# Products that nobody reads in TensorE's waits, and the late queries projected ahead of the first scores

## The chip, the cores and the metric

The kernel runs on one core of a Trainium2 chip. The metric is device microseconds per execution. Before the change three runs took 763.17, 768.37 and 766.54 us, a median of 766.54.

## The reference, cut to what matters

Four batches of 256 tokens of width 256 pass two layers. Each layer is a cross-attention and a routed feed-forward block, all added to the residual `x`:

```
x = x + L0_xattn(layernorm(x), ctx, pos)   # 32 heads of 8, rotary angles on q and k
x = x + L0_ffn(layernorm(x))               # 16 experts of 128, top 2 of 2 groups, plus a shared expert of 512
x = x + L1_xattn(layernorm(x), ctx)        # 16 heads of 16, per-head layernorm of q and k, two softmaxes added
x = x + L1_ffn(layernorm(x))               # 60 experts of 176, top 4, plus a gated shared expert of 704
```

The result is the final `x`, in float32. Nothing of the computation changes.

## The kernel before, in words

Tokens are eight tiles of 128 (`NT`), and each stage is one block in which the five engines run their own programs and meet on semaphores; a stage starts when all engines have ended the one before. `ps` is the accumulator memory of eight banks, named by number.

**Preparation and first attention** share a block. `prep_l0` (L237) multiplies the context by the key and value weights (L302: two float32 products per tile, 16 in all), turns the key by its angles on VectorE and GpSimd (L362, L368, L411), then transposes (L177) and projects (L197) the eight normed tiles for the queries, and turns those in the same way. Before the third key tile TensorE waits until the first has been turned; before the third query tile (`t == 2`) it waits for the first turned query. Keys and queries are split into three bf16 parts per value (`split_tensor` L223, then ScalarE, VectorE, GpSimd), the parts are written to memory and read back as stacks, first by SyncE and the last two splits by ScalarE's queue.

`attention` (L492) serves both layers. Its first loop on TensorE computes the first eight pairs of score products (`scores`, L629), runs at most three pairs ahead of VectorE's maxima (L769), and behind the fourth pair transposes the negated maxima of the first unit (`transposed_maxima`, L642), which SyncE then puts behind the queries (L555). A product with a zero row (L733) clears bank 6. The main loop, one step per pair of heads, issues scores eight pairs ahead, the shifted scores (L659), whose exponentials ScalarE takes (L857), the values (L674) and the turned sums (`token_sums`, L687). In the last steps the normalised rows are transposed and projected (`transposed`, `projected`, through L177 and L197), and VectorE adds them to `x` with statistics (L801, L803).

**Routing and experts of the first layer** (`route_and_experts_l0`, L916): VectorE norms, TensorE transposes eight tiles (L177, two banks in turn with ScalarE's copies L190), multiplies by the router's 16 columns (L197), then runs the shared expert (L1001, L1011) and 32 units of routed experts (L1041, L1052). GpSimd squares the hidden values (L1131, L1141); ahead of its first square it waits for small loads and copies masks (L1118).

**The second attention** begins with what the first could not do earlier: the queries of the last four tiles (`LateQueries`, L1515). VectorE norms them, TensorE turns two tiles (L1538) and projects them (L197), and VectorE adds the bias and centres (L1601), sums squares (L1607), spreads and scales (L1613 to L1621); TensorE transposes the result (L1554), and VectorE takes the rest (L1467). TensorE's list interleaves this with pairs 1 and 2 of the scores; VectorE's list interleaves it with the maxima. In TensorE's program before:

```
for n in range(AHEAD * UP):
    ...
    if late is not None and 1 <= n <= 2:
        late.tensor_turned(pe, n - 1)
    scores(n, 0)
    scores(n, 1)
    if late is not None and 1 <= n <= 2:
        late.tensor_projected(pe, n - 1)
```

**Routing and experts of the second layer** (`route_shared_l1`, `routed_l1`): eight transposes of pairs (L177), the gate product of 61 columns (L197), three units of the shared expert's first product (L1874, four products of 512 columns each), one of its second (L1889, L1890), and then the ranks (L1898), which need VectorE's mask of the chosen experts (L2036). The routed experts, their loads and the final sum follow from there.

The order on every engine is written out by hand. SyncE issues almost all loads. No planner is involved.

Of the kernel before, what the change touches and what calls it, by code (L numbers as in the profile page):

```python
# [18 lines left out]
P = 128  # L19
# [22 lines left out]
def bcast(ap, axis, n):  # L42

    a = ap.unsqueeze(axis)
    shape = list(a.shape)
    shape[axis] = n
    return a.broadcast_to(shape)
# [143 lines left out]
                          m.ps[:, bank, 0:D].rearrange("p (c t) -> p c t", c=KD))  # L191


def matmul_tile(nc, out, xT, i, w, bias=None, ones=None):

    for c in range(KD):
        ins = nc.tensor.matmul(out, xT[:, c, i * P:(i + 1) * P], w[:, c, :], start=(c == 0),  # L197
                               stop=(c == KD - 1 and bias is None))
    if bias is not None:
        ins = nc.tensor.matmul(out, ones, bias, start=False, stop=True)  # L200
    return ins
# [35 lines left out]
def prep_l0(nc, m, io, block, ctx):  # L237

    lay = L0
# [53 lines left out]
    @block.tensor  # L293
    def _(pe):
        pe.wait_ge(ld_ctx, 16)
        pe.wait_ge(ld_wkv, 16)
        for i in range(NT):
            if i >= 2:
                pe.wait_ge(v_copied, i - 1)
                pe.wait_ge(rot_ready, i - 1)  # L300
            for side in range(2):
                ins = nc.tensor.matmul(ps[:, 2 * side + i % 2, 0:D], m.ctxT[:, i * P:(i + 1) * P],  # L302
                                       wkv[:, side * D:(side + 1) * D], start=True, stop=True)
            ins.then_inc(kv_ps, 1)
        pe.wait_ge(v_copied, NT)
        pe.wait_ge(ld_const, 32)
        pe.wait_ge(ld_wq, 16)
        for i in range(NT + 1):
            if i == 3:
                for s in K_SPLITS:  # L310
                    split_tensor(nc, pe, m, s, rot_done, rest_ready).then_inc(split_ps, 1)
            if i == 6:
                for s in Q_SPLITS[0:2]:
                    split_tensor(nc, pe, m, s, rot_done, rest_ready).then_inc(split_ps, 1)
            if i < NT:
                pe.wait_ge(xn_ready, i + 1)
                if i >= 2:
                    pe.wait_ge(xt_ready, i - 1)
                transpose_tile(nc, m, 2 + i % 2, m.xn[:, i, :]).then_inc(xt_ps, 1)
            if i >= 1:  # L320
                t = i - 1
                pe.wait_ge(xt_ready, t + 1)
                if t >= 2:
                    pe.wait_ge(rot_ready, NT + t - 1)
                matmul_tile(nc, ps[:, 4 + t % 2, 0:D], m.xT, t, wq).then_inc(q_ps, 1)
        for s in Q_SPLITS[2:4]:
            split_tensor(nc, pe, m, s, rot_done, rest_ready).then_inc(split_ps, 1)

# [163 lines left out]
def attention(nc, m, lay, io, block, w_dram, b_dram, v_bias=None, late=None):  # L492
# [12 lines left out]
    UP = G // 2  # L505
# [5 lines left out]
    with ExitStack() as ctx:  # L511
# [100 lines left out]
        def _(pe):  # L612
# [92 lines left out]
            def projected(i):  # L705
# [4 lines left out]
                    pe.wait_ge(out_used, i)  # L710
                matmul_tile(nc, ps[:, out_bank(i) + 1, 0:D], m.xT, i, ow).then_inc(out_ps, 1)

            for n in range(AHEAD * UP):
                if lay is L0 and n == 2:
                    pe.wait_ge(m.rest_ready, len(SPLITS))
                if late is not None and 1 <= n <= 2:
                    late.tensor_turned(pe, n - 1)
                scores(n, 0)
                scores(n, 1)
                if late is not None and 1 <= n <= 2:  # L720
                    late.tensor_projected(pe, n - 1)
                if n == UP:
                    if late is not None:
                        pe.wait_ge(late.cent, 2)
                    transposed_maxima(0)
                if late is not None and n == UP:
                    pe.wait_ge(negT_ready, 1)
                    for k in range(2):
                        late.tensor_split(pe, k)
            if late is not None:  # L730
                pe.wait_ge(late.rest_ready, 2)
            pe.wait_ge(zero_row_set, 1)
            nc.tensor.matmul(ps[:, 6, :], m.ones_row[:], zero_row, start=True, stop=True)  # L733
            pe.wait_ge(ones_ld, 16 * RT * NBUF)
            for n in range(PAIRS + TURN_LAG + 1):
                if n + AHEAD * UP < PAIRS:
                    scores(n + AHEAD * UP, 0)
                if n < PAIRS:
                    shifted_scores(n)
                if n + AHEAD * UP < PAIRS:  # L740
                    scores(n + AHEAD * UP, 1)
                if n < PAIRS:
                    if n % UP == 0 and n // UP + 1 < U:
                        transposed_maxima(n // UP + 1)
                if n >= LAG and (n - LAG + 1) % (CT // 2) == 0 and n - LAG < PAIRS:
                    values((n - LAG + 1) // (CT // 2) - 1)
                if turn_at(n) is not None:
                    token_sums(turn_at(n))
                if 0 < n - OUT <= NT - 2:
                    projected(n - OUT - 1)  # L750
                if 0 <= n - OUT < NT - 2:
                    transposed(n - OUT)
            for i in (NT - 2, NT - 1):
                transposed(i)
            for i in (NT - 2, NT - 1):
                projected(i)

        @block.vector
        def _(dve):
# [44 lines left out]

            if late is not None:
                late.vector_norm(dve, chain)
            for n in range(AHEAD * UP):
                maxima(n)
                if late is not None:
                    if n in (1, 2):  # L810
                        late.vector_biased(dve, n - 1)
                    if n in (2, 3):
                        late.vector_summed(dve, n - 2)
                    if n == UP - 1:
                        late.vector_spread(dve, chain)
                    if n == UP + 1:
                        for k in range(2):
                            late.vector_rest(dve, k)
                if n % UP == UP - 1:
                    negated(n // UP)  # L820
                if late is not None and n == UP - 1:
                    late.vector_scaled(dve, chain)
# [93 lines left out]
def route_and_experts_l0(nc, m, io):  # L916

    with ExitStack() as ctx:
# [71 lines left out]

        @block.tensor
        def _(pe):
            transpose_and_project(nc, pe, m, xn_ready, xt_ps, xt_ready, rw, E0, logit_ps, 6, ld, 64)

            def hidden(n):
# [103 lines left out]
            for n in range(UNITS0):  # L1099
                if n + 1 < UNITS0:  # L1100
                    routed_hidden(n + 1)
                routed_outputs(n)
                keys(n)
                queries(n)

        @block.gpsimd
        def _(pool):
# [686 lines left out]
def route_shared_l1(nc, m, io, block, ctx):  # L1794
# [67 lines left out]
    def _(pe):  # L1862
# [42 lines left out]
        def table(i):  # L1905
# [3 lines left out]
                                       start=(i == 0 and j == 0), stop=(i == NT - 1 and j == TOP1 - 1))  # L1909
            ins.then_inc(table_ps, 1)  # L1910

        for i in range(NT):
            pe.wait_ge(xn_ready, i + 1)
            if i >= 2:
                pe.wait_ge(xt_ready, i - 1)
            transpose_tile(nc, m, 4 + i % 2, m.xn[:, i, :]).then_inc(xt_ps, 1)
# [559 lines left out]
```

## Time and profile before

| what | value |
|---|---|
| median of three runs | 766.54 us |
| the profiled execution's own time | 768.52 us |
| its span | 766.6 us |
| TensorE busy | 646.2 us (84%) |
| VectorE busy | 425.9 us (56%) |
| ScalarE busy | 297.3 us (39%) |
| GpSimd busy | 259.2 us (34%) |
| mean granted TensorE clock | 0.898 of full |

The span runs from the first instruction to the last; 1.9 us of the execution's own time lie around it. In the rows PE is TensorE, PEld its weight loads, DVE VectorE, ACT ScalarE, POOL GpSimd, SP SyncE. A float32 product that is not a transposition appears as two records in every row here (line 302 makes 16 products and has 32 records), a transposition as one. A granted clock of 1.00 is 2.4 GHz and 0.50 is 1.2 GHz; a value between is a mean over the stretch.

### The profile page before, as it was taken

How to read it: one execution, taken by the hardware profiler on the slowest of the kernel's cores; microseconds unless marked ns; L12 is line 12 of the kernel's file. 1: busy time of each engine (PE TensorE's matmuls, PEld its weight loads, DVE VectorE, ACT ScalarE, POOL GpSimd, SP SyncE). 2: the span in 40 equal slices, each digit the busy share in tenths (PEclk: the TensorE clock that was granted, in tenths of full speed). 3: DMA queues.
4: the chain of work that ended last, by engine and by line, in shares of the span. 5: the costliest groups of instructions: out<-in, count | busy, mean ns of one | idle time of the engine just before them, and what ended most of it. 6: DMA issues, size and time to landing. Idle time of an engine off the chain costs nothing. (4 is left out here: it accounts for less than half of the span.)

```text
span 766.6 us, 12462 instructions
## 1 busy us (share of the span) xinstructions
PE 646.2 (84%) x4224; PEld 388.7 (51%) x4224; DVE 425.9 (56%) x1130; ACT 297.3 (39%) x552; POOL 259.2 (34%) x403
## 2 busy tenths in 40 slices
PE   1657988887799999999569999599999999999750
PEld 1542444444566666676335556365666555555330
DVE  4668788863330767967687564448982222222116
ACT  1332777785323122423036667342214232232110
POOL 5350011111135323313101333302258677777140
PEclk9895899998599999999779999759999999999875
DMA  3086122100600464553914310099001899999907
GB/s 116 1 277 197 45 64 64 45 2 1 175 0 1 127 182 151 166 179 97 240 32 126 85 45 2 12 276 245 4 12 36 236 290 276 271 269 279 266 32 274
DMA packets 82615, 99.59 MB, mean 130 GB/s; under 512 B 11610, under 2 KB 58049, under 8 KB 82547
## 3 DMA queue, kind: packets, MB, share of 16 engines
q1 hardware_dynamic: 74738, 86.53, 39.9%
q0 software_dynamic: 5600, 8.53, 4.3%
q10 hardware_dynamic: 2208, 3.67, 1.3%
q8 instruction: 36, 0.59, 0.3%
q14 instruction: 33, 0.26, 0.1%
HBM read 82.42 MB, written 21.63 MB: 136 GB/s over the span
## 5 line engine op out<-in xcount | busy, mean ns | idle before, releaser
L769 DVE TENSOR_REDUCE l_mx<-ps 128x2 f32<-128x512 f32 (+2 forms) x256 | 125.9, 550 | 46.7 <-PE ps L629 46.4
L857 ACT ACTIVATE l_prob<-ps 128x1024 f32<-128x1024 f32 x96 | 98.4, 1026 | 27.0 <-PE ps L659 26.8
L629 PE MATMUL ps<-l_ks,l_qs 48*128 48x256 bf16 (+1 forms) x384 | 73.1, 305 | 26.4 <-DMA l_qs<-l_q_stacks 13.2
L1392 DVE SCALAR_TENSOR_TENSOR xs<-ps,comb,xs 128x256 f32<-128x256 f32 x128 | 55.8, 482 | 59.5 <-PE ps L1052 59.4
L674 PE MATMUL ps<-l_prob,v 128*9 128x256 f32 (+1 forms) x768 | 71.4, 395 | 1.1 <-ACT l_prob L857 1.1
L2146 POOL DMA_INDIRECT y_rows<-r_sw,row x53 | 53.4, 1008 | 44.3 <-DVE r_sw L2287 33.6
L2280 DVE TENSOR_TENSOR r_hot<-r_hot,ps 128x352 f32<-128x352 f32 (+1 forms) x35 | 15.1, 432 | 95.1 <-ACT r_hot L2255 95.1
L1141 POOL TENSOR_TENSOR r_ehid<-r_erelu 128x512 f32<-128x512 f32 x32 | 35.5, 1109 | 83.6 <-ACT r_erelu L1245 83.5
L1790 POOL DMA_INDIRECT xg<-x_rows,r_empty x53 | 56.2, 1060 | 19.9 <-issue 10.5
L1052 PE MATMUL ps<-f_w,r_ehid 128*128 128x256 f32 x256 | 60.8, 381 | 0.2
L1041 PE MATMUL ps<-xT,f_w 128*128 128x512 f32 x128 | 60.0, 593 | 0.0
L629 PEld LDWEIGHTS ps<-l_ks,l_qs 48*128 48x128 bf16 (+1 forms) x384 | 30.1, 103 | 58.0 <-issue 21.8
L1052 PEld LDWEIGHTS ps<-f_w,r_ehid 128*128 128x128 f32 x256 | 48.5, 190 | 21.0 <-issue 13.9
L659 PE MATMUL ps<-l_qs,l_ks 50*128 50x256 bf16 (+1 forms) x384 | 57.6, 285 | 0.0
L597 POOL TENSOR_TENSOR attn<-rest,l_rec 128x32 f32<-128x32 f32 x64 | 14.4, 246 | 115.0 <-DVE l_rec L788 115.0
L597 POOL TENSOR_TENSOR l_ctxv<-rest,l_rec 128x64 f32<-128x64 f32 x64 | 17.6, 296 | 84.6 <-DVE l_rec L788 84.6
L2255 ACT ACTIVATE r_hot<-ps 128x352 f32<-128x352 f32 (+1 forms) x35 | 13.7, 392 | 79.8 <-PE ps L2184 79.8
L1874 PE MATMUL ps<-xT,r_sw 128*128 128x512 f32 x88 | 42.2, 621 | 0.0
L2287 DVE TENSOR_SCALAR r_sw<-ps,row_w 128x256 f32<-128x256 f32 x53 | 24.0, 481 | 30.1 <-PE ps L2205 30.1
L674 PEld LDWEIGHTS ps<-l_prob,v 128*9 128x9 f32 (+1 forms) x768 | 27.2, 99 | 23.4 <-issue 10.2
L2184 PE MATMUL ps<-ew,r_at_low 128*64 128x352 f32 (+1 forms) x304 | 38.3, 465 | 0.1
L2184 PE MATMUL ps<-ew13b,r_at_low 128*64 128x352 f32 (+1 forms) x240 | 33.3, 478 | 5.4 <-DMA ew2b<-in_L_w 5.4
(278 smaller groups left out, 1110.4 us busy)
## 6 DMA issues: line engine op xcount, KB each, us to landing
ew<-in_L_w SPq DMA_DIRECT2D x18, 704.0 KB, 8.1
ew13b<-in_L_w SPq DMA_DIRECT2D x12, 704.0 KB, 10.9
f_w<-in_L_w SPq DMA_DIRECT2D x32, 256.0 KB, 2.7
ew<-in_L_w SPq DMA_DIRECT2D x18, 384.0 KB, 9.8
ew2b<-in_L_w SPq DMA_DIRECT2D x12, 384.0 KB, 13.9
ew13b<-in_L_w SPq DMA_DIRECT2D x12, 352.0 KB, 13.1
l_k_stacks<-part SPq DMA_DIRECT2D x8, 384.0 KB, 3.3
l_ks<-l_k_stacks SPq DMA_DIRECT2D x32, 96.0 KB, 2.2
```

The costliest lines, as they stand in the source:

```text
L629: ins = nc.tensor.matmul(ps[:, score_bank(n) + k, qt * S:(qt + 1) * S], qs[row:row + R, u % NBUF, col, qt * P:(qt + 1) * P], ks[row:row + ...
L659: ins = nc.tensor.matmul(ps[:, 2 + 2 * (n % 2) + k, kt * S:(kt + 1) * S], ks[row:row + lay.krows, b, col, kt * P:(kt + 1) * P], qs[row:row ...
L674: ins = nc.tensor.matmul(ps[row:row + W, 6, (c % 2) * S:(c % 2 + 1) * S], v[:, n // UP // GR * QT + kt, head, :], prob[:, n % PROBS, k, kt ...
L769: ins = nc.vector.reduce_max(mx[:, u % 2, :, s, head], one[:, :, lo:hi], AX_X)
L857: nc.scalar.activation(prob[:, n % PROBS, :, :, :].rearrange("p h k q -> p (h k q)"), ps[:, 2 + 2 * (n % 2):4 + 2 * (n % 2), :].rearrange( ...
L1041: ins = nc.tensor.matmul(m.ps[:, n % 2, :], m.f0_up[:, n % WSLOTS, c, :], m.xT[:, c, half * HT:(half + 1) * HT], start=(c == 0), stop=(c = ...
L1052: nc.tensor.matmul(m.ps[:, 2 + t, 0:D], ehid[:, n % 2, t * P:(t + 1) * P], m.f0_down[:, n % WSLOTS, :], start=True, stop=True).then_inc(e_ ...
L1392: v.scalar_tensor_tensor(m.xs[:, i, :], m.ps[:, 2 + t, 0:D], m.comb[:, i, e:e + 1], m.xs[:, i, :], ALU.mult, ALU.add).then_inc(e_added, 1)
L1790: nc.gpsimd.indirect_dma_start(m.xg[:, b % XBUF, :], None, m.x_rows, bass.IndirectOffsetOnAxis(m.token[:, b:b + 1], 0), bounds_check=T - 1 ...
L1874: ins = nc.tensor.matmul(ps[:, 2 * (q % 2) + a, :], sw13[:, k, own], m.xT[:, k, h * TILES * P:(h + 1) * TILES * P], start=(k == 0), stop=( ...
L2146: nc.gpsimd.indirect_dma_start(m.y_rows, bass.IndirectOffsetOnAxis(m.row[:, b:b + 1], 0), yb[:, b % YBUF, :], None, bounds_check=ROWS - 1, ...
L2184: ins = nc.tensor.matmul(ps[row:row + n, spot(b), 0:2 * I1], xgT[:, spot(b), c * P + row:c * P + row + n], w13[:, s, c, :], start=(c == 0) ...
```

## The change

A helper issues float32 products of the identity by itself, twice side by side, so 128 by 256 outputs, into a bank that nobody reads at that time. It has no semaphore. Calls of it are put on TensorE's list at these places: 30 before the third key tile (with the wait for the identity's load moved ahead of them), 15 before the third query tile's projection, 7 before the last two splits; 15 ahead of the first attention's scores, 8 (second attention: 11) ahead of the first transposed maxima, 2 ahead of the zero row, 2 in each of the three last steps of the loop, 5 before the last two transposed tiles and 5 after their projection; 8 at the start of the first routing, 6 at the end of the first experts; 9 at the start of the second routing. In the second attention the late queries are taken out of the loop: 9 products, both turnings, 3 products, a projection, 3 products, the other projection, 3 products, and then the scores; 5 more products stand ahead of the late splits. On VectorE both biases come ahead of the first maxima, and the sums and the spread one pair earlier.

```diff
+def keep_running(nc, m, bank, count):
+    for _ in range(count):
+        nc.tensor.matmul(m.ps[:, bank, 0:2 * P], m.ident[:], bcast(m.ident[:], 1, 2), start=True, stop=True)
...
         for i in range(NT):
+            if i == 2:
+                pe.wait_ge(ld_const, 32)
+                keep_running(nc, m, 4, 30)
             if i >= 2:
                 pe.wait_ge(v_copied, i - 1)
                 pe.wait_ge(rot_ready, i - 1)
...
         pe.wait_ge(v_copied, NT)
-        pe.wait_ge(ld_const, 32)
         pe.wait_ge(ld_wq, 16)
...
                 pe.wait_ge(xt_ready, t + 1)
+                if t == 2:
+                    keep_running(nc, m, 2, 15)
                 if t >= 2:
                     pe.wait_ge(rot_ready, NT + t - 1)
...
+        keep_running(nc, m, 2, 7)
         for s in Q_SPLITS[2:4]:
...
+            if late is None:
+                keep_running(nc, m, 2, 15)
+            else:
+                keep_running(nc, m, 2, 9)
+                for p in range(2):
+                    late.tensor_turned(pe, p)
+                keep_running(nc, m, 2, 3)
+                for p in range(2):
+                    late.tensor_projected(pe, p)
+                    keep_running(nc, m, 2, 3)
             for n in range(AHEAD * UP):
                 if lay is L0 and n == 2:
                     pe.wait_ge(m.rest_ready, len(SPLITS))
-                if late is not None and 1 <= n <= 2:
-                    late.tensor_turned(pe, n - 1)
                 scores(n, 0)
                 scores(n, 1)
-                if late is not None and 1 <= n <= 2:
-                    late.tensor_projected(pe, n - 1)
                 if n == UP:
                     if late is not None:
                         pe.wait_ge(late.cent, 2)
+                    keep_running(nc, m, 6, 8 if lay is L0 else 11)
                     transposed_maxima(0)
                 if late is not None and n == UP:
                     pe.wait_ge(negT_ready, 1)
+                    keep_running(nc, m, 6, 5)
                     for k in range(2):
                         late.tensor_split(pe, k)
...
+            keep_running(nc, m, 6, 2)
             nc.tensor.matmul(ps[:, 6, :], m.ones_row[:], zero_row, start=True, stop=True)
...
+                if n >= PAIRS:
+                    keep_running(nc, m, 2, 2)
                 if turn_at(n) is not None:
                     token_sums(turn_at(n))
...
+            keep_running(nc, m, 2, 5)
             for i in (NT - 2, NT - 1):
                 transposed(i)
             for i in (NT - 2, NT - 1):
                 projected(i)
+            keep_running(nc, m, 2, 5)
...
                 late.vector_norm(dve, chain)
+                for p in range(2):
+                    late.vector_biased(dve, p)
             for n in range(AHEAD * UP):
                 maxima(n)
                 if late is not None:
-                    if n in (1, 2):
-                        late.vector_biased(dve, n - 1)
-                    if n in (2, 3):
-                        late.vector_summed(dve, n - 2)
-                    if n == UP - 1:
+                    if n in (0, 1):
+                        late.vector_summed(dve, n)
+                    if n == 2:
                         late.vector_spread(dve, chain)
...
+            keep_running(nc, m, 2, 8)     # route_and_experts_l0, ahead of transpose_and_project
...
+            keep_running(nc, m, 0, 6)     # route_and_experts_l0, behind the last unit
...
+        keep_running(nc, m, 2, 9)         # route_shared_l1, ahead of the transposes
```

## Rows read from the trace of the kernel before

**Rows 1.** The page's forty slices: granted TensorE clock, tenths of full.
```profile
PEclk9895899998599999999779999759999999999875
```

**Rows 2.** Windows: length, busy us (records) of PE, PEld, DVE, ACT, POOL, then PEclk, DMA.
```profile
9.20:13.00 3.80, 3.74 (x8) 2.52 (x8) 2.98 (x11) 0.58 (x2) 2.37 (x2) 1.00 0.07 18
...
33.40:36.80 3.40, 2.22 (x20) 1.91 (x18) 1.48 (x3) 2.40 (x5) 0.56 (x1) 1.00 0.00 0
...
69.10:81.20 12.10, 11.39 (x88) 5.04 (x90) 8.22 (x18) 6.81 (x9) 0.00 (x0) 0.50 0.23 64
...
498.10:515.10 17.00, 16.12 (x55) 11.34 (x56) 6.60 (x19) 7.65 (x13) 0.00 (x0) 0.51 0.98 276
```

**Rows 3.** The chain that ended last: start, us, work; late in the second routing.
```profile
545.92 1.73 PE ps L1890 x8
```

**Rows 4.** Timeline of TensorE, 0 to 60: start, us, work, records, [idle before].
```profile
21.34 6.24 PE L302 MATMUL ps<-attn,ctxT_sb 128*128 128x256 f32 x16 [8.34 <-DVE k_tm L368]
...
39.92 1.82 PE L197 MATMUL ps<-attn,xT 128*128 128x256 f32 x4 [4.29 <-DVE q_tm L368]
...
43.84 1.03 PE L197 MATMUL ps<-attn,xT 128*128 128x256 f32 x4
...
53.02 1.09 PE L223 MATMUL ps<-ident,q_tm 128*128 128x128 f32 x8 [1.89 <-POOL q_tm L411]
58.22 3.79 PE L629 MATMUL ps<-l_ks,l_qs 48*128 48x256 bf16 x20 [4.11 <-DMA l_qs<-l_q_stacks]
```

**Rows 5.** Timeline of VectorE at the first attention's first maxima.
```profile
58.87 4.88 DVE L769 TENSOR_REDUCE l_mx<-ps 128x2 f32<-128x512 f32 x8 [3.25 <-PE ps L629]
```

**Rows 6.** Timeline of ScalarE, first attention: exponentials of steps 0, 6 and 63.
```profile
70.22 1.02 ACT L857 ACTIVATE l_prob<-ps 128x1024 f32<-128x1024 f32 x1 [3.85 <-PE ps L659]
...
81.75 1.04 ACT L857 ACTIVATE l_prob<-ps 128x1024 f32<-128x1024 f32 x1
...
182.20 1.02 ACT L857 ACTIVATE l_prob<-ps 128x1024 f32<-128x1024 f32 x1 [0.82 <-PE ps L659]
```

**Rows 7.** Timeline of TensorE, end of the first attention and first routing.
```profile
187.95 1.11 PE L177 MATMUL ps<-ident,attn 128*128 128x128 f32 x4 [1.55 <-POOL attn L597]
...
202.09 7.01 PE L197 MATMUL ps<-r_rw,xT 128*128 128x16 f32 x32 [0.46 <-ACT xT L190]
...
215.08 1.24 PE L1011 MATMUL ps<-r_sdown,r_hid 128*128 128x256 f32 x5
```

**Rows 8.** Timeline of VectorE and GpSimd, the same stretch.
```profile
193.37 0.43 DVE L803 BATCH_NORM_STATS2 bn<-xs 128x6 f32<-128x256 f32 x1
...
209.27 2.58 POOL L1118 COPY v<-r_pmask 128x16 f32<-128x16 f32 x16 [14.18 <-DMA r_vb<-in_L_vb_T]
...
213.41 1.04 POOL L1131 TENSOR_TENSOR r_hid<-r_relu 128x512 f32<-128x512 f32 x1 [1.56 <-ACT r_relu L1172]
```

**Rows 9.** Timeline of TensorE, start of the second attention.
```profile
377.14 1.03 PE L629 MATMUL ps<-l_ks,l_qs 96*128 96x256 bf16 x4 [9.09 <-DMA l_qs<-l_q_stacks]
...
390.29 0.27 PE L642 MATMUL ps<-ident_bf,l_neg 128*32 128x128 bf16 x2 [3.65 <-DVE l_neg L779]
...
400.46 0.58 PE L629 MATMUL ps<-l_ks,l_qs 96*128 96x256 bf16 x2 [0.68 <-DVE l_mx L769]
```

**Rows 10.** VectorE: end of first experts, a bias (timeline), the first maxima (window).
```profile
368.49 1.40 DVE L1398 BATCH_NORM_STATS2 bn<-xs 128x6 f32<-128x256 f32 x4
...
382.63 0.69 DVE L1601 TENSOR_TENSOR q_tm<-ps,qw 128x512 f32<-128x512 f32 x1 [1.72 <-PE ps L197]
...
377.70:390.20 12.50, 8.64 (x43) 6.62 (x40) 9.21 (x26) 2.71 (x7) 0.00 (x0) 0.85 0.78 172
```

**Rows 11.** Timeline of TensorE, second routing up to the ranks.
```profile
503.36 7.09 PE L197 MATMUL ps<-r_gw,xT 128*128 128x61 f32 x32 [0.46 <-ACT xT L190]
...
525.53 0.19 PE L1898 MATMUL ps<-r_mask_bf,r_upper_bf 128*128 128x60 bf16 x1
```

**Rows 12.** Timeline of VectorE, the mask in the second routing.
```profile
523.22 0.66 DVE L2036 TENSOR_TENSOR r_mask_bf<-r_logit,r_prob 128x480 bf16<-128x480 f32 x1
```

## The prediction

> **What bounds the kernel now.** I began with the page's forty slices of granted clock [rows 1]: a slice is 19.2 us, and below 9 lie slices 2, 4 and 5, 10 and 11, 20 and 21, 26 and 27: dips at the starts and ends of both attentions and in both routings (the last three slices belong to the end, which the change leaves alone). Windows then show each dip: the key products have the full 2.4 GHz before the wait, the first loop steps stand at 1.2 GHz (0.50 for 12.1 us), and so does the second routing (0.51 for 17.0 us), although TensorE is busy 94 to 95% of both [rows 2]. So a dip is paid after the wait, as long as TensorE itself is late. TensorE's timeline gives the waits (the last number of a row) and what released them [rows 4, 7, 9, 11]; VectorE's, GpSimd's and ScalarE's give who else is late [rows 5, 6, 8, 10, 12]. The chain of waits covers only the last block, from 494.5 on, so the other stages are read from timelines.
>
> **What is added.** 168 unread products. Each is float32, 256 columns, as L1890's; its eight records, four products, took 1.73 us at the full clock, 0.43 each [rows 3]. Key-tile products of that shape, slower, took 6.24 us for eight, 0.78 each [rows 4]; the first four took 3.74 us, 0.94 each, though the window reads 1.00 [rows 2]. I take 0.43 wherever TensorE has just been busy, since products themselves keep it busy. The question at each place is whether count times 0.43 is shorter than the wait, for TensorE runs its list in order: a product that outlasts the wait delays everything behind it. No DMA is moved or added. The moved wait for the identity's load costs nothing: the load is one of the first of the block, and in 9.2 to 13.0 DMA moves only a 0.07 share [rows 2].
>
> **1. Preparation and first attention: +4.7.** Thirty products are 13.0 us from 13.0 (21.34 less the wait of 8.34): 26.0, so key tile 2 is 4.6 late [rows 4]. In exchange the key products come at the full clock; of the stretch 21.3 to 26.5, half its TensorE time less the waits on VectorE's turning, I take 2.2 back: +2.4. Fifteen are 6.5 against a wait of 4.29: 2.2 more. Of the four-record projections behind them the first takes 1.82 (a second, two us on, as long) and the one at 43.84, where the clock is back, 1.03 [rows 4]; two such savings, 1.6, come back: +3.0 for part 1 so far. Seven are 3.0 against 1.89, +1.1, but these splits go by ScalarE's queue and their loads land at 58.22 now, so about 61.2 to 62.3 then. The 15 products behind the splits (splits end at 54.11 [rows 4], plus 3.0 plus 1.1, plus 6.5) end at 64.2 to 64.7: they, not the load, release the first scores, 6.0 later. Then VectorE's maxima set the pace (4.88 for four pairs [rows 5]), whatever the clock of the scores. Eight products, 3.5, put the transposed maxima 0.9 behind their release, most of it covered by VectorE. The first exponential is +6.0. Loop steps 0 to 6 then took 11.53 (70.22 to 81.75); the later 57 took 100.45, 1.76 each, so six at the full clock are 10.57, a gain of 0.96 [rows 6]; the other bound is 2.0, if the late start finds the queue full. I take 1.3: **+4.7**.
>
> **2. End of that attention, first routing: −1.6.** Three times two and five products are 4.75 us in the waits ahead of the last transposed tiles, of which the last is 1.55 before 187.95 [rows 7]: from 0 to 1.85 late, I take 1.35. The transposes and projections behind are at half clock; half their time gives 2.2: −0.85. Five products behind the projection end near 194.06, VectorE's last statistics at 193.80 [rows 8] less 0.85: the block's end waits for TensorE, +0.25. In the routing the logits (7.01 [rows 7]) halve, but the routing is not freed by as much: GpSimd copies masks until 211.85, released by a DMA, not by TensorE, and only then squares (1.04 [rows 8]). So the first output is at about 213.2 instead of 215.08 [rows 7]: −1.9 and +0.25.
>
> **3. Start of the second attention: +0.6.** Six products begin at 368.05 (377.14 less 9.09 [rows 9]) and end at 370.65; VectorE ended at 369.89 [rows 10]: the block starts 0.75 later. The first scores now stand behind 18 products (7.8), eight transposes (1.1, as at 53.02 [rows 4]) and 16 projection records (eight products, 3.5): 383.1 for 377.14, +5.9. What that costs is set by VectorE: its work ahead of the negated maxima was 9.21 busy in 377.7 to 390.2 [rows 10], of which the biases and sums go ahead (two biases, 0.69 each [rows 10]); 7.8 to 8.3 after the first maxima at 383.5 gives 391.7. Eleven products begun when the scores are issued end at 392.1, against 390.29 [rows 9]: +1.8. The prologue ends near 400.46 [rows 9] plus 1.5, and the first loop steps at the full clock give back 0.9. The hoisting is paid by the scores, repaid by VectorE's shorter list: near zero.
>
> **4. End of that attention, second routing: −5.2.** The block starts 0.95 later, an estimate from part 2's terms: products at the same four places of the tail, with less returned. Nine products, 3.9, put the eight transposes 1.2 behind, but at the full clock these end as before, and the logits begin at 503.35 [rows 11]. They halve, 7.09 to 3.55. Then TensorE has the shared expert, some 24 products of 0.43 and a second product of 1.7 to 2.7 (L1890's records are 1.73 [rows 3]): 503.35 + 3.5 + 10.3 + 2.7 = 519.9 at most. The ranks need VectorE's mask, ready at 523.88 [rows 12], which follows the logits: 523.88 − 3.55 = 520.3. That binds: ranks at 520.35 for 525.53 [rows 11], −5.2. The routed experts behind them move with the ranks, as do their loads.
>
> **Sum.** 4.7 − 1.6 + 0.6 − 5.2 = −1.5 on the execution's own 768.5: 767.0. That execution lies 2.0 above the median of the runs shown, so 765. Bounds of this case: lowest, −1.6 for blocks that do not wait for products, −2.0 for larger loop gains, and −3 for a prep that gives back more, 758; highest, +1.5 where the first thirty products begin below full clock, +1 for the start of the second attention, +2.5 for smaller returns, 770.
>
> **A rule against the row.** In 33.4 to 36.8 eighteen of TensorE's twenty records are transposes, and the clock stays 1.00 [rows 2]. I therefore let transposes hold the clock in parts 2 to 4. The Trainium skill, "TensorE: Matmul & The Clock Gate", section "Part 4: PE-mode transpose", says otherwise: transposes do not count as busy for the clock. By that rule the sum would be near +7.6, and the row does not bear it out.
>
> **Rivals.**
> *The clock is lost again in the transposes and narrow logits* (slower side). Place: both routings, between the eight or nine products and the shared expert. The 1.2 GHz then stays, the logits take their 7.0, and the products are only late: second routing +1.25 for −5.2, first routing 2.7 worse. −1.5 + 6.45 + 2.7 = +7.65 on the median: 774. It decides if the clock falls before the logits are half done. Against: 33.4 to 36.8 [rows 2]; for: no row shows 16 or 61 columns at the full level after a wait. That stretch is short and follows on products. Chance 0.15.
> *A product costs one record, 0.216 us* (faster side). Then 30 are 6.5 against 8.34, 15 are 3.2 against 4.29 and 4.11, 7 are 1.5 against 1.89 [rows 4], eleven 2.4 against 3.65 [rows 9]: every group ends inside its wait, nothing is late, and only the gains stay: about −6 in part 1 (2.2 + 1.6 + 1.3 and the projections), −3.7, −3.5 and −7.3: −20, 747. Against: L1890 has eight records for four products [rows 3], and L302 sixteen for eight; for: no row has an operand read twice over. Chance 0.13.
> *Nothing changes*, the products not holding the clock at all: late starts without returns, which is the first rival and worse, near 780; 0.02, since the same shape of product does hold it in the rows.
>
> **Chances and range.** Forecast 0.70, rivals 0.15, 0.13, 0.02. One per cent, what a measurement of this kernel can tell from no change, is 7.7 us: faster is below 758.9, slower above 774.2. The forecast's own range, 758 to 770, gives 0.07 to faster and 0.63 to same; the clock rival, at the edge, is split between same (0.05) and slower (0.10). Faster 0.20, same 0.68, slower 0.12. The range goes from 752, under the forecast's low end by what gains seen only in part may add, to 774: it leaves out the cheap product and half of the slower rival, 2 in 10.
>
> **What would show it.** Granted clock 1.00 in 13 to 35, 58 to 87, 187 to 215, 372 to 407 and 488 to 515 if the products hold it. 336 records of the new line if a product is two; 168 and 0.216 each would be the cheap one. Key tile 2 near 26.0, first scores of the first attention near 64.5, its first exponential near 76; transposed maxima of the second attention 1.8 later against its block's start plus 0.75; the distance from the logits' start to the ranks 17.0 instead of 22.2. The forecast is wrong if the preparation's products are shown ahead of the release they stand beside (then part 1 is a gain), or if a clock at 0.5 follows them (then part 4 is none).

## The result, and the profile after

The changed kernel takes 778.36 us (median of four runs, 775.49 to 782.17) where the kernel before, with one more run beside the three known, takes 764.86: a ratio of 1.0174, 95% interval [1.0133, 1.0216]. It is slower, and the prediction, 765 within 752 to 774, was wrong. The profiled execution is 778.18 with a span of 776.3, 9.7 us more than the profiled one of before.

Line numbers are those of the changed kernel: L197 is the unread product (336 records, two each), L311 the keys, L640 the scores, L881 the exponentials, L203 the small projections, L1900 and L1916 the second layer's shared expert, L1924 the ranks. First the page's granted clock by slices, against [rows 1]: the dips of the second, fourth and eleventh slice are gone, but a 7 stands in the fifth and in the twenty-second.

```profile
PEclk9999799999989999999997999989999999999875
```

Windows (columns as in [rows 2]) show where the clock is lost again: among the eight products ahead of the transposed maxima, in the first loop steps, in the logits of the first routing, around the second attention's zero row, and in the logits of the second routing and the shared expert behind them.

```profile
13.40:27.40 14.00, 14.00 (x61) 12.14 (x60) 8.23 (x34) 1.34 (x4) 1.02 (x2) 1.00 0.00 0
69.10:74.40 5.30, 5.30 (x17) 4.11 (x16) 3.64 (x9) 0.00 (x0) 0.00 (x0) 0.68 0.73 198
79.50:91.30 11.80, 11.03 (x88) 4.66 (x86) 8.14 (x16) 7.41 (x11) 0.00 (x0) 0.57 0.22 61
211.90:217.20 5.30, 5.30 (x32) 5.30 (x33) 0.00 (x0) 1.24 (x1) 0.00 (x0) 0.66 0.86 280
405.00:412.00 7.00, 5.26 (x19) 2.66 (x17) 5.83 (x17) 3.86 (x5) 0.00 (x0) 0.72 0.00 1
515.40:520.50 5.10, 5.06 (x32) 5.09 (x33) 0.65 (x5) 0.89 (x1) 0.00 (x0) 0.69 1.11 347
520.50:533.00 12.50, 12.50 (x27) 5.27 (x26) 11.07 (x37) 5.62 (x9) 2.67 (x2) 0.85 1.07 302
```

TensorE's timeline, against [rows 4, 9, 11] (start, us, work, records, idle before):

```profile
13.42 14.19 PE L197 MATMUL ps<-ident 128*128 128x256 f32 x60
27.45 1.89 PE L311 MATMUL ps<-attn,ctxT_sb 128*128 128x256 f32 x8
...
39.59 6.64 PE L197 MATMUL ps<-ident 128*128 128x256 f32 x30
...
59.24 6.64 PE L197 MATMUL ps<-ident 128*128 128x256 f32 x30
65.82 0.83 PE L640 MATMUL ps<-l_ks,l_qs 48*128 48x256 bf16 x12
...
69.10 5.41 PE L197 MATMUL ps<-ident 128*128 128x256 f32 x16
74.44 0.28 PE L653 MATMUL ps<-ident_bf,l_neg 128*16 128x128 bf16 x2
...
224.02 1.99 PE L1036 MATMUL ps<-r_sdown,r_hid 128*128 128x256 f32 x8 [1.54 <-POOL r_hid L1157]
...
392.16 1.69 PE L640 MATMUL ps<-l_ks,l_qs 96*128 96x256 bf16 x14
...
408.13 2.07 PE L197 MATMUL ps<-ident 128*128 128x256 f32 x4 [1.74 <-DVE rest L1493]
410.13 2.07 PE L753 MATMUL ps<-l_prob,ones_row 1*128 1x512 f32 x2
...
515.44 5.32 PE L203 MATMUL ps<-r_gw,xT 128*128 128x61 f32 x32 [0.87 <-DMA r_starts<-in_starts]
520.56 12.32 PE L1900 MATMUL ps<-xT,r_sw 128*128 128x512 f32 x24
...
535.47 0.19 PE L1924 MATMUL ps<-r_mask_bf,r_upper_bf 128*128 128x60 bf16 x1
```

And ScalarE's exponentials of steps 0 and 6, against [rows 6], then GpSimd's mask copies, against [rows 8]:

```profile
79.55 1.02 ACT L881 ACTIVATE l_prob<-ps 128x1024 f32<-128x1024 f32 x1 [3.13 <-PE ps L670]
...
91.28 1.03 ACT L881 ACTIVATE l_prob<-ps 128x1024 f32<-128x1024 f32 x1
...
220.66 2.32 POOL L1144 COPY v<-r_pmask 128x16 f32<-128x16 f32 x16 [15.31 <-DMA r_vb<-in_L_vb_T]
```

Stage by stage, the later kernel's mark less the earlier one's (VectorE's first instruction of a block marks its start):

| mark | before | after | difference |
|---|---|---|---|
| first key product | 9.26 | 9.88 | +0.6 |
| first scores, first attention | 58.22 | 65.82 | +7.6 |
| first exponential | 70.22 | 79.55 | +9.3 |
| last exponential | 182.20 | 191.70 | +9.5 |
| first outputs, first routing | 215.08 | 224.02 | +8.9 |
| start of the second attention | 370.18 | 379.98 | +9.8 |
| its first exponential | 401.93 | 413.63 | +11.7 |
| start of the second routing | 494.56 | 507.07 | +12.5 |
| ranks | 525.53 | 535.47 | +9.9 |
| end | 766.6 | 776.3 | +9.7 |

Nearly all is lost before the first exponential. Against the medians of 764.86 and 778.36 the loss is 13.5: the profiled execution of before lies 3.7 above its median, and no stage can be named for these 3.7.

### The profile page after: what moved, and what is told of

It reads as the page before. It is cut to its first block and busy times, and to the rows that moved or that the text cites. A ratio compares the mean times of both kernels' runs of the same rounds, so it can differ in the third digit from the quotient of the medians.

```text
span 776.3 us, 13130 instructions
## 1 busy us (share of the span) xinstructions
PE 696.6 (90%) x4560; PEld 439.0 (57%) x4560; DVE 424.6 (55%) x1130; ACT 297.0 (38%) x552; POOL 259.4 (33%) x403
## 5 line engine op out<-in xcount | busy, mean ns | idle before, releaser
L881 ACT ACTIVATE l_prob<-ps 128x1024 f32<-128x1024 f32 x96 | 98.6, 1028 | 28.3 <-PE ps L670 28.1
L197 PE MATMUL ps<-ident 128*128 128x256 f32 x336 | 81.2, 395 | 3.7 <-DVE rest L1493 1.7
L640 PE MATMUL ps<-l_ks,l_qs 48*128 48x256 bf16 (+1 forms) x384 | 68.0, 282 | 15.8 <-DVE l_mx L793 12.0
L197 PEld LDWEIGHTS ps<-ident 128*128 128x128 f32 x336 | 64.9, 198 | 15.4 <-issue 3.9
L640 PEld LDWEIGHTS ps<-l_ks,l_qs 48*128 48x128 bf16 (+1 forms) x384 | 28.0, 97 | 45.9 <-issue 21.9
L1900 PE MATMUL ps<-xT,r_sw 128*128 128x512 f32 x88 | 41.8, 616 | 0.0
## 6 DMA issues: line engine op xcount, KB each, us to landing
ew13b<-in_L_w SPq DMA_DIRECT2D x12, 704.0 KB, 15.2
```

The source lines that it names most:

```text
L197: nc.tensor.matmul(m.ps[:, bank, 0:2 * P], m.ident[:], bcast(m.ident[:], 1, 2), start=True, stop=True)
L640: ins = nc.tensor.matmul(ps[:, score_bank(n) + k, qt * S:(qt + 1) * S], qs[row:row + R, u % NBUF, col, qt * P:(qt + 1) * P], ks[row:row + ...
L881: nc.scalar.activation(prob[:, n % PROBS, :, :, :].rearrange("p h k q -> p (h k q)"), ps[:, 2 + 2 * (n % 2):4 + 2 * (n % 2), :].rearrange( ...
L1900: ins = nc.tensor.matmul(ps[:, 2 * (q % 2) + a, :], sw13[:, k, own], m.xT[:, k, h * TILES * P:(h + 1) * TILES * P], start=(k == 0), stop=( ...
```

## The experiments

Kernels of one set ran on one chip beside the kernel before (766.44, 764.18 and 766.09 us in sets one to three). Intervals are 95%. Theory A: the products outlast their waits, and the clock they buy is lost again. Its rivals stand in the expectations.

**Set one. The hoisting alone**: every count is 0.

```diff
-                keep_running(nc, m, 4, 30)
+                keep_running(nc, m, 4, 0)
```

> All products are left out; the late queries stay ahead of the second attention's first scores. Theory A (the products outlast the waits they stand in, and the full clock they buy is lost again in the next thin stretch): without them the first attention ends as in the kernel before, the second attention's first scores come some 4 to 5 us later than before because the turnings and projections run at 1.2 GHz, VectorE's shorter list takes most of that back: +0.5 to +2 us against the kernel before, 765 to 767. Rival B (the hoisting itself is the loss): +8 to +13. Rival C (the hoisting is a gain that the products hide): -2 to -4.

Measured 761.51, ratio 0.9942 [0.9903, 0.9981]. Rival C: the hoisting is a gain, and it was hidden by the products; 4.9 below the kernel before is a little more than its 2 to 4. From the block's start to the second attention's first transposed maxima it is 18.0 us (368.32 to 386.35), 20.1 before (370.18 to 390.29), and to the next block's start 121.1, 124.4 before. The kernel with the fitted preparation, below, has the same list there and took 18.5 and 121.7. So some 3 us of the gain are the second attention's. Another 1.5 of the profile's difference stand in steps 0 to 6 of the first attention (10.05 for 11.53), where nothing is changed. The first scores come 2.4 later against that start, but all that follows goes by VectorE's list, which has lost its waits for the projections.

```profile
377.70 2.00 PE L640 MATMUL ps<-l_ks,l_qs 96*128 96x256 bf16 x14
...
386.35 0.37 PE L653 MATMUL ps<-ident_bf,l_neg 128*32 128x128 bf16 x2 [4.08 <-DVE l_neg L803]
```

**Without the first stage's products** (30, 15, 7, 15, 8 become 0, all else as changed):

```diff
-                    keep_running(nc, m, 6, 8 if lay is L0 else 11)
+                    keep_running(nc, m, 6, 0 if lay is L0 else 11)
```

> The groups of 30, 15, 7 and 15 products and the 8 ahead of the first transposed maxima of the first attention are left out; all other products and the hoisting stay. Theory A: the first exponential is back at its old place (70.2, not 79.6), and of the 9 us that the profiles differ by nearly all goes: -8 to -10 us against the changed kernel, 768 to 770. Rival B (the hoisting, or the second layer, carries the loss): -1 to -4.

Measured 770.32, ratio 1.0056 [1.0016, 1.0096]; the first exponential is at 70.92. So the first stage carries 8 us of the loss (9 by the ratios), as theory A has it; but 770 is still 9 above the hoisting alone, so the later products cost too.

**Counts that fit the waits**: (30, 15, 7, 15) become (17, 9, 4, 9), and the rest likewise.

```diff
-                keep_running(nc, m, 4, 30)
+                keep_running(nc, m, 4, 17)
...
-                keep_running(nc, m, 2, 9)
+                keep_running(nc, m, 2, 6)
```

> Every group is cut so that count times 0.45 us is no longer than the wait it stands in (17, 9, 4, 9; 5 and 9 ahead of the transposed maxima; 1 per step; 3 or 4, 2; 6, 4; 6, 2, 1, 1; 1; 8). Theory A, sizes are all that is wrong: the first attention ends 2 to 4 us earlier than before, the routings gain 1 to 3 together: -3 to -7 us against the kernel before, 758 to 762. Rival D (the clock falls again behind each group whatever its size, and the stages are set by VectorE and by loads): -2 to +2, 763 to 767.

Measured 755.08, ratio 0.9850 [0.9781, 0.9919], a gain larger than expected. Other counts make a difference of some 23 us. In the profile the first routing's block starts 5.5 sooner than before (188.55 for 194.10): 2.3 of it stand at the first exponential, 1.5 in steps 0 to 6, and 1.9 between the last exponential and that start (9.99 us; 11.90 before, 12.65 changed). The second attention's first exponential is 27.94 behind its block's start, 3.8 less than before, of which the hoisting alone gave 2.2.

**Transposes in place of the thirty products**, one execution (772.35):

```diff
-                keep_running(nc, m, 4, 30)
+                keep_turning(nc, m, 4, 120)   # nc.tensor.transpose(ps, ident, ident), 128 columns
```

> As the changed kernel, but the thirty products ahead of key tile 2 are replaced by 120 transposes of the identity, the same time at the full clock. If transposes hold the clock as the stretch 33.4 to 36.8 of the kernel before suggested: granted clock 1.00 in 13 to 27, about 13 us for the 120, key products behind them at 1.9 us for eight records. If they do not: the clock falls to 0.5 within the stretch, the transposes take 14 to 26 us, and the key products behind them start at 1.2 GHz (about 3.4 us for eight records).

They hold the clock: 120 take 13.97 us, and it reads 1.00 to the end of the stretch. By the rule of the Trainium skill, "TensorE: Matmul & The Clock Gate", "Part 4: PE-mode transpose", it would have fallen; here it does not, so the measurement decides.

```profile
13.45 13.97 PE L202 MATMUL ps<-ident 128*128 128x128 f32 x120
27.26 1.89 PE L316 MATMUL ps<-attn,ctxT_sb 128*128 128x256 f32 x8
```

```profile
24.00:27.00 3.00, 3.00 (x30) 3.00 (x29) 0.00 (x0) 0.00 (x0) 0.00 (x0) 1.00 0.00 0
```

**Set two. Narrow products in place of the thirty**, one execution (785.78):

```diff
-                keep_running(nc, m, 4, 30)
+                keep_narrow(nc, m, 4, 60)     # ident by ident[:, 0:16]
```

> As the changed kernel, but the thirty products ahead of key tile 2 are replaced by 60 products of 16 columns, as wide as the first router's logits. If narrow products hold the clock: granted clock 1.00 in 13 to 27 and some 0.22 us for each (two records of 0.11), as half of the 7.01 us that 16 of them took at 1.2 GHz gives. If they lose it: 0.5 from within the stretch on, up to 0.44 us each, and the key products behind start at 1.2 GHz.

They lose it, back to back, with TensorE busy throughout:

```profile
13.00:17.00 4.00, 4.00 (x35) 4.00 (x34) 3.59 (x20) 1.48 (x4) 0.00 (x0) 1.00 0.00 0
17.00:21.00 4.00, 4.00 (x22) 4.00 (x21) 3.86 (x14) 0.22 (x1) 0.00 (x0) 0.53 0.00 0
21.00:25.00 4.00, 4.00 (x21) 4.00 (x20) 1.15 (x4) 0.00 (x0) 1.01 (x2) 0.50 0.02 4
```

So products as narrow as the logits lose the clock with no gap between them. In the routings that is not the whole cause. There the transposes ahead of the logits stand with gaps of 0.2 to 0.5 us, and in the fitted kernel the clock was at 0.5 nearly from the start of the second logits, behind a last wait of 1.49:

```profile
491.40:492.80 1.40, 0.00 (x0) 0.00 (x0) 0.06 (x1) 1.38 (x3) 0.00 (x0) 1.00 1.02 316
492.80:494.00 1.20, 1.14 (x6) 1.17 (x6) 0.67 (x5) 0.28 (x1) 0.00 (x0) 0.52 1.09 382
```

```profile
492.86 7.05 PE L203 MATMUL ps<-r_gw,xT 128*128 128x61 f32 x32 [1.49 <-DMA r_starts<-in_starts]
```

**Products between the routings' transposes** (in both, with 2 more ahead of the second router's weights; none ahead of the first attention's maxima and zero row):

```diff
             transpose_tile(nc, m, 4 + i % 2, m.xn[:, i, :]).then_inc(xt_ps, 1)
+            if i % 2 == 1:
+                keep_running(nc, m, 2, 1)
+        keep_running(nc, m, 2, 2)
```

> The fitted kernel with one product behind every second transposed tile of both routings, two more ahead of the wait for the second router's weights, and none ahead of the first attention's first transposed maxima and zero row. If it is the short idle gaps between the transposes that lose the clock: granted clock near 1.00 through both logits, each about 3.6 us for 32 records instead of 6.6 and 7.1, the ranks 3 to 4 us nearer the block's start, and 750 to 753 in all. If the narrow logits lose it by themselves: the clock still falls within them, 5 to 7 us each, and 754 to 757.

Measured 756.51, ratio 0.9869 [0.9801, 0.9938]. By the clock it is the first case of the expectation, by the time the second. Both logits run at the full clock (3.75 and 3.69 us; 6.62 and 7.05 in the fitted kernel).

```profile
195.71 3.75 PE L203 MATMUL ps<-r_rw,xT 128*128 128x16 f32 x32
...
497.21 3.69 PE L203 MATMUL ps<-r_gw,xT 128*128 128x61 f32 x32
```

Over all kernels, the logits took 3.68 to 3.78 us in all five routings with products between the transposes and in three of the seventeen with products only ahead of them; in the other fourteen they took 4.89 to 7.05. One of these three is the second routing of the kernel with eight products ahead of the loop (below), whose list there is the fitted kernel's:

```profile
495.82 3.78 PE L203 MATMUL ps<-r_gw,xT 128*128 128x61 f32 x32 [0.46 <-ACT xT L190]
```

So the products between the transposes hold the clock through the logits; without them the same list of a routing kept it in one kernel and lost it in another. The gaps have a part in the loss; how large the narrow products' part is in the routings, the runs do not show.

In the first routing the held clock is worth nothing here: its first outputs come 20.06 us after the block's start, 20.31 in the fitted kernel, because GpSimd's copies wait for the load; TensorE idles 5.90, loses the clock, and what follows runs at 1.2 GHz. The next fourteen records take 2.9 us more than in the fitted kernel, and the experts' block ends that much later.

```profile
199.30 3.68 PE L1026 MATMUL ps<-xT,r_sup 128*128 128x512 f32 x8
208.88 3.78 PE L1036 MATMUL ps<-r_sdown,r_hid 128*128 128x256 f32 x8 [5.90 <-POOL r_hid L1157]
```

```profile
208.80:213.30 4.50, 4.42 (x10) 3.53 (x11) 0.18 (x1) 0.00 (x0) 1.08 (x2) 0.50 0.00 0
```

**The fitted preparation alone, with the hoisting**:

```diff
-                keep_running(nc, m, 4, 30)
+                keep_running(nc, m, 4, 17)    # 9, 4, 9 at the next three places; 0 elsewhere
```

> Hoisting, and only the four fitted groups of the preparation and the first attention's start (17, 9, 4, 9); no other product. Theory A2 (the hoisting gives some 4 us in the second layer, the fitted preparation some 3 more, each by itself): first scores at about 55 instead of 58, the second attention as with the hoisting alone: 757 to 760, -2 to -4 against the hoisting alone. Rival E (the gain of the fitted kernel comes from the routings and the second attention's products): no difference from the hoisting alone, 761 to 762.

Measured 763.26, ratio 0.9975 [0.9940, 1.0010]: no gain beyond the hoisting can be told, and it lies above both ranges of the expectation. In its profile the first scores are 3.1 sooner (55.08), but steps 0 to 6 of the loop take 12.10 us instead of 11.53, and the first outputs are only 2.4 sooner than before. What this kernel lacks beside the fitted one in the first attention's end is seen too: 11.90 us from the last exponential to the next block, as before.

**Eight products just ahead of the loop**, one execution (758.50):

```diff
-            keep_running(nc, m, 6, 2 if lay is L0 else 0)
+            keep_running(nc, m, 6, 8 if lay is L0 else 0)
```

> The fitted kernel with the 5 products ahead of the first attention's first transposed maxima left out and 8 instead of 2 ahead of the zero row, just before the loop. They delay the loop by 1 to 3 us. If the first steps are slow by the clock alone, and it holds: the exponentials of steps 0 to 6 take 10.6 us instead of 11.5. If something else sets the steps: 11.3 or more with a granted clock near 1.00. If the clock falls again within them: 0.5 to 0.7 in those steps and 11.3 or more.

Nearest to the third case: the clock is 0.78 in 68.5 to 74.0 and 0.64 in 74.0 to 80.0, and steps 0 to 6 take 11.03 (69.01 to 80.04). It falls within the steps. Over all kernels these steps took 10.02 to 12.10, and the clock in them goes with the time: 0.72 to 0.74 in the four that took 10.02 to 10.05, 0.51 to 0.57 in those of 11.5 and more. The list does not decide which it is. The kernel before and the hoisting alone have no products there and took 11.53 and 10.05; the first two kernels of set three have the same list up to the second routing's ranks and took 11.81 and 10.04 (first rows: before and hoisting alone; then those two):

```profile
70.20:81.80 11.60, 10.96 (x87) 4.76 (x86) 7.95 (x16) 7.41 (x11) 0.00 (x0) 0.53 0.18 48
69.90:80.00 10.10, 8.99 (x86) 4.02 (x86) 7.80 (x16) 7.29 (x11) 0.00 (x0) 0.74 0.20 57
...
67.30:79.20 11.90, 11.22 (x88) 4.80 (x86) 7.96 (x16) 7.41 (x11) 0.00 (x0) 0.55 0.22 60
67.00:77.10 10.10, 9.18 (x86) 4.02 (x86) 7.80 (x16) 7.31 (x11) 0.00 (x0) 0.72 0.23 62
```

So 1.5 us of the difference between any two profiles can come from here. What decides it from one execution to the next stays open.

**Set three. The counts that the profiles speak for** (fitted; products between the second routing's transposes only; none ahead of the first attention's maxima, the zero rows and the late splits), from the fitted kernel:

```diff
-                    keep_running(nc, m, 6, 5 if lay is L0 else 9)
+                    keep_running(nc, m, 6, 0 if lay is L0 else 9)
...
-                    keep_running(nc, m, 6, 1)
+                    keep_running(nc, m, 6, 0)
...
-            keep_running(nc, m, 6, 2 if lay is L0 else 0)
+            keep_running(nc, m, 6, 0)
...
             transpose_tile(nc, m, 4 + i % 2, m.xn[:, i, :]).then_inc(xt_ps, 1)
+            if i % 2 == 1:
+                keep_running(nc, m, 2, 1)
+        keep_running(nc, m, 2, 2)
```

> The fitted kernel with what the profiles so far speak for: one product behind every second transposed tile of the second routing alone and two ahead of its weights' wait; none ahead of the first attention's transposed maxima, ahead of the zero row and ahead of the late splits. Theory F (a gain counts where TensorE sets the stage's end): first attention and second attention as in the fitted kernel or 0.5 to 1 us sooner, the ranks 27 to 27.5 us after the block's start instead of 30.4; 751 to 755, -1.4 to -1.9% against the kernel before. Rival G (the routed experts' loads set the end): the same ranks, but 755 to 757.

Measured 753.37, ratio 0.9843 [0.9800, 0.9885]: faster than both kernels and within theory F's range. The ranks come 27.65 us after the block's start, 30.97 before, 28.40 changed.

```profile
493.01 3.68 PE L203 MATMUL ps<-r_gw,xT 128*128 128x61 f32 x32
496.53 10.52 PE L1900 MATMUL ps<-xT,r_sw 128*128 128x512 f32 x24
...
510.77 0.20 PE L1924 MATMUL ps<-r_mask_bf,r_upper_bf 128*128 128x60 bf16 x1 [0.96 <-DVE r_mask_bf L2066]
```

**The ranks held back**:

```diff
             pe.wait_ge(mask_ready, 1)
+            keep_running(nc, m, 6, 12)
```

> The last kernel with twelve more products between the wait for the mask and the ranks, 5.2 us of TensorE in the second routing with nothing beside them. If everything behind the ranks moves with them, as the prediction had it: +4 to +5.5 us against the last kernel. If the routed experts' loads or other slack behind the ranks set the end: 0 to +2.

Measured 760.06, 6.7 above the last kernel, more than the 4 to 5.5 expected, for products that take 5.45 us. In the profiles the ranks come 32.77 us after the block's start instead of 27.65. What is behind the ranks moves with them, and no load or slack takes it up. The products hold back all that follows on TensorE's list too, so the run does not tell the ranks from the list.

```profile
508.51 5.45 PE L197 MATMUL ps<-ident 128*128 128x256 f32 x24 [0.79 <-DVE r_mask_bf L2067]
513.80 0.19 PE L1925 MATMUL ps<-r_mask_bf,r_upper_bf 128*128 128x60 bf16 x1
```

**The hoisting undone in the set's first kernel** (18 products in one group ahead of the scores):

```diff
-                keep_running(nc, m, 2, 6)
...
+                keep_running(nc, m, 2, 18)
...
+                if late is not None and 1 <= n <= 2:
+                    late.tensor_turned(pe, n - 1)
```

> The first kernel of this set with the hoisting undone on TensorE and VectorE (turnings and projections between pairs 1 and 2 again, biases and sums at their old places), and 18 products ahead of the first scores in one group, which fit the old wait of 9 us. If the hoisting is worth what it gave alone: the second attention's loop starts 2 to 4 us later, +2 to +4 us in all. If the clock held by products makes it needless: within 1 us.

Measured 756.33, ratio 0.9872 [0.9834, 0.9910], 3.0 above it; the intervals overlap. In the profiles the second attention's first exponential stands 29.86 us after the block's start instead of 28.00, and the stage takes 122.0 instead of 119.2 (118.8 with the ranks held back). The hoisting is worth about 3 here too.

**Three groups less in the changed kernel**, one execution (779.38):

```diff
-                    keep_running(nc, m, 6, 8 if lay is L0 else 11)
+                    keep_running(nc, m, 6, 0 if lay is L0 else 11)
...
-                    keep_running(nc, m, 6, 5)
+                    keep_running(nc, m, 6, 0)
...
-            keep_running(nc, m, 6, 2)
+            keep_running(nc, m, 6, 0)
```

> The changed kernel with three of its groups left out: the 8 ahead of the first attention's transposed maxima, the 2 ahead of both zero rows, the 5 ahead of the late splits. If these are what the sum missed behind the first scores (2.2 us in the first attention between its first scores and first exponential, 1.9 in the second's prologue): the first exponential 12.0 us behind the first scores instead of 13.7, and the second attention's loop 1.5 to 2 us sooner against its block's start. If the falling clock takes it all the same: 13 or more, and no change in the second.

The first exponential is 11.77 us behind the first scores (13.73 changed, 12.00 before), and the second attention's first exponential 30.92 behind the block's start (33.65 changed): these groups were the 2 us in the first place. In the second they were 1.2 to 2.7, since two other kernels with the changed list there took 32.10 and 32.36. The whole execution is no shorter, since from ranks to end it took 247.7 us; in the others that was 235.8 to 245.2, and why one execution differs so from another there was not settled.

```profile
64.30 0.83 PE L640 MATMUL ps<-l_ks,l_qs 48*128 48x256 bf16 x12
...
76.07 1.02 ACT L881 ACTIVATE l_prob<-ps 128x1024 f32<-128x1024 f32 x1 [3.85 <-PE ps L670]
```

## Why the prediction was wrong

The mechanism of the price was right: products are two records each, run one after the other and outlast their waits. Two steps failed: that a clock once won would last until the work it was meant for, and that products in the prologues of both attentions cost nothing or are covered. Every part missed in the same direction; by the profiles the sum was 9.7 for −1.5, of which 0.6 is the first load's landing.

- **Part 1, +4.7: measured +8.9.** The price was low: 0.47 us a product in the first group (14.19 for 30), which the prediction had as a bound of its range, and 0.44 in the next, for 0.43; with the waits between, first scores came 7.0 later against the first key product, for 6.0 to 6.5. The eight products ahead of the maxima were to be late by 0.9, "most of it covered by VectorE"; they took 5.41, not 3.5, because the clock fell under them (0.68), and 1.7 went to the first exponential. The gain of 1.3 in the loop did not come: steps 0 to 6 took 11.73, with the clock at 0.57 again. The failed step is that a clock once won would last through scores that VectorE paces. That these steps take 10.0 or 11.5 with one and the same list (set two) could not be seen in the one trace of before. The key products gave back what was forecast (2.0 for 2.2).
- **Part 2, −1.6: measured −0.6 up to the first outputs.** The block started 0.75 later, where +0.25 was forecast: the products of the tail made it 12.65 us long from the last exponential for 11.90, and with fewer of them it was 9.99. GpSimd's copies bound the rest, as the prediction had it, but they stand 16.3 us behind the block's start for 15.2 before: the load landed later, so 1.3 came back and not 1.9.
- **Part 3, +0.6: measured +2.8.** The block's start was right (+0.9, with the experts), and the transposed maxima were too: 1.0 later against it, as forecast (1.8 less 0.75). Missed were the two products ahead of the second zero row: they stand behind the wait for VectorE, with nothing beside them, and took 2.07 at 1.2 GHz. No term of the sum had them, nor the five ahead of the splits. The 0.9 that the loop's first steps were to give back did not come: from the first exponential to the last it is 78.63, 78.71 before. That the hoisting is near zero was wrong: alone it is a gain of 2 us up to the first exponential and 3 in the whole stage, since VectorE's list sets the transposed maxima.
- **Part 4, −5.2: measured −2.0.** The logits took 5.32 for 3.55 and the shared expert 12.32, little less than the 12.70 before: the clock fell within the narrow logits. Place and cause are the first rival's, at a chance of 0.15: transposes back to back hold the clock, but the routings' stand with gaps, and products in these gaps kept it. The size of the step was nearly right where the clock held: in the four kernels whose second logits ran at the full clock the ranks come 25.97 to 27.65 behind the block's start, 3.3 to 5.0 sooner than before, and the end goes with the ranks.

So the first rival came true in part: the clock was lost in both routings, about half-way through the logits. That and the uncovered products put the time beyond its 774. The forecast had also taken 2.0 off because the profiled execution of before lay that far above its median; that of the changed kernel lies on its own (778.18 for 778.36).

## What to carry to other kernels

Unread products are a price on TensorE's list: count times the measured duration must stay below the wait, group by group, and a group behind a semaphore wait has no cover at all. Fill only waits behind which TensorE itself sets the stage's end; where a load or VectorE did here, the clock was lost again before it could be used. Fill the short gaps behind a long wait too, up to the work that is to gain. Look at each stage's own marks, over more than one execution: counts fitted place by place, with the hoisting, turned a loss of 1.7% into a gain of 1.6%.

## What the runs showed of the hardware

- Sixty products of 16 columns lost the full clock though TensorE had no gap; 120 transposes of 128 columns held it for 13.97 us. That the two differ so was not expected.
- At 1.00 granted the 16-column records took 0.11 us each on the mean of the first 4.0 us (35); at 0.50 about 0.19 (21 in 4.0).
- The first eight key records took 3.75 us under a window that reads 1.00, while eight later ones took 1.89: the price of the very first products is not shown by the granted clock.
